# Both routers with the gate weights stationary, the output bias of the experts on VectorE, row transfers without holds, and the output stored by group

## The reference

```
logits = xf @ router_w.T
probs = jax.nn.sigmoid(logits.astype(jnp.float32))
topw, sel = jax.lax.top_k(probs, TOP_K)
combine = jnp.sum(topw[:, :, None] * onehot, axis=1)
h = jnp.square(jax.nn.relu(jnp.einsum('td,edw->tew', xf, W1e)))
out = jnp.einsum('ted,te->td', jnp.einsum('tew,ewd->ted', h, W2e), combine)
```

```
gates = jax.nn.softmax(xf @ wg, axis=-1)
idx = jnp.argmax(gates, axis=-1)
keep = loc < cap
disp = zeros.at[slot].set(xf, mode='drop')
h = jnp.einsum('ecd,edf->ecf', disp, w1) + b1[:, None, :]
y = jnp.einsum('ecf,efd->ecd', h, w2) + b2[:, None, :]
out = jnp.where(keep[:, None], gate_val[:, None] * y[slot], 0.0)
y2 = _ln(y1 + out, ln2_g, ln2_b)
```

## Time and profile before

| | |
|---|---|
| median of 3 runs | 2754.14 us |
| the profiled execution | 2750.36 us, of it 2748.6 us from the first to the last record (the span) |
| TensorE (PE) busy | 2386.5 us, 87% |
| its weight loads (PEld) | 1706.0 us, 62% |
| VectorE (DVE) busy | 1222.7 us, 44% |
| ScalarE (ACT) busy | 1013.9 us, 37% |
| GpSimd (POOL) busy | 146.0 us, 5% |
| mean granted TensorE clock | 0.959 of 2.4 GHz |
| DMA | 74.82 MB, 27 GB/s over the span |

### The profile page before, as it was taken

One profiled execution on the slowest core, in us unless ns is written; L12 is line 12 of the kernel. 1 busy time (PEld: TensorE's weight loads), 2 busy tenths in 40 slices (PEclk: granted clock), 3 DMA queues, 4 the chain that ended last, 5 costly groups with the idle time before them and its releaser, 6 DMA issues. The chain is left out here.

```text
span 2748.6 us, 38901 instructions
## 1 busy us (share of the span) xinstructions
PE 2386.5 (87%) x15301; PEld 1706.0 (62%) x15301; DVE 1222.7 (44%) x2353; ACT 1013.9 (37%) x2866; POOL 146.0 (5%) x238
## 2 busy tenths in 40 slices
PE   6778887999988999989999999978998997874894
PEld 4455655666655666666666666656876765654773
DVE  5456665777764434333333333345344443331003
ACT  3245564777762111113333333343223443331122
POOL 0000000000000000000000000021001000002003
PEclk8989999999999999999999999999999999996996
DMA  3000001000002000020000000000001000012332
GB/s 113 16 1 1 1 1 39 13 24 13 24 11 82 1 1 0 1 109 8 8 9 9 8 9 1 1 28 1 0 25 57 16 9 16 1 57 75 115 119 65
DMA packets 52535, 74.82 MB, mean 27 GB/s; under 512 B 8051, under 2 KB 41349, under 8 KB 51205
## 3 DMA queue, kind: packets, MB, share of 16 engines
q1 hardware_dynamic: 50820, 68.14, 7.4%
q0 software_dynamic: 1536, 4.20, 0.6%
HBM read 63.94 MB, written 8.39 MB: 26 GB/s over the span
## 5 line engine op out<-in xcount | busy, mean ns | idle before, releaser
L856 ACT ACTIVATE ca_prob<-bank,ca_nmax 128x512 f32<-128x512 f32 x256 | 174.0, 690 | 93.1 <-DVE ca_nmax L922 93.1
L922 DVE TENSOR_REDUCE ca_nmax<-bank 128x1 f32<-128x512 f32 x256 | 164.2, 683 | 56.3 <-PE bank L714 56.2
L856 ACT ACTIVATE na_prob<-bank,na_nmax 128x257 f32<-128x257 f32 x256 | 117.9, 473 | 180.9 <-DVE na_nmax L922 180.9
L1446 PE MATMUL bank<-XN,rf_W 128*128 128x512 f32 x384 | 171.8, 598 | 0.0
L1457 PE MATMUL bank<-rf_W,rf_h 128*128 128x256 f32 x768 | 170.8, 379 | 0.0
L1457 PEld LDWEIGHTS bank<-rf_W,rf_h 128*128 128x128 f32 x768 | 145.9, 190 | 33.1 <-issue 14.8
L728 PEld LDWEIGHTS bank<-cst,ca_prob 128*128 128x128 f32 x1024 | 112.3, 142 | 73.7 <-issue 63.3
L856 ACT ACTIVATE ra_prob<-bank,ra_nmax 128x256 f32<-128x256 f32 x256 | 118.2, 482 | 104.1 <-DVE ra_nmax L922 104.1
L1501 ACT ACTIVATE rf_r<-bank 128x512 f32<-128x512 f32 x96 | 57.4, 598 | 255.3 <-PE bank L1446 255.3
L728 PE MATMUL bank<-cst,ca_prob 128*128 128x128 f32 x1024 | 140.5, 279 | 6.6 <-DVE ca_pT L928 5.9
L922 DVE TENSOR_REDUCE na_nmax<-bank 128x1 f32<-128x257 f32 x256 | 90.8, 417 | 118.2 <-PE bank L714 118.2
(11 more groups left out here) (399 smaller groups left out, 4505.8 us busy)
## 6 DMA issues: line engine op xcount, KB each, us to landing
xl_w<-in_L_ffn_w SPq DMA_DIRECT2D x16, 1024.0 KB
dp_cx<-in_ctx_tok SPq DMA_DIRECT2D x4, 1024.0 KB, 14.8
ca_v<-in_ctx_values SPq DMA_DIRECT2D x8, 512.0 KB, 4.5
rf_W<-in_L_ffn_w SPq DMA_DIRECT2D x8, 512.0 KB, 8.7
na_Wkv<-in_L_xattn_Wkv SPq DMA_DIRECT2D x1, 4096.0 KB
na_cxT<-in_ctx SPq DMA_DIRECT2D x8, 512.0 KB, 3.4
ma_cxT<-in_ctx SPq DMA_DIRECT2D x8, 512.0 KB, 3.4
X<-in_x SPq DMA_DIRECT2D x1, 2048.0 KB, 7.6
```

The lines of the kernel that those rows point to most:

```text
L856: e = act.activation(prob[:, n % 2, u, hh * keys:(hh + 1) * keys], S[u][:, hh * keys:(hh + 1) * keys], ACT.Exp, bias=nmax[:, n % 2, u, hh: ...
L922: v.tensor_reduce(nmax[:, n % 2, u], S[u][:, 0:W].rearrange("p (h k) -> p h k", h=per), AX.X, ALU.max, negate=True).then_inc(maxed, 1)
L1446: mm = pe.matmul(g.bank[n % 3][:], W1[:, k, c * P:(c + 1) * P], g.XN[:, k, gi * GT:(gi + 1) * GT], start=(k == 0), stop=(k == KD - 1))
```

## The change

1. **Routed feed-forward.** The router weights are loaded into a tile of 32 columns that GpSimd has filled with zeros (SP waits for that fill, `blank`, before its first load). One `route()` for all tokens: the weights are the stationary side, 512 tokens the moving one, and group gi goes to the partitions 32 gi of bank 4. ScalarE copies the bank to `lgT`, TensorE transposes it after `hidden(0)` (`turn_logits`), and one `take()` gives the exponentials of all groups. The three later `route` calls are gone.
2. **Expert layer, gate.** The same form (`lgT`, its four transposes after q = 1); ScalarE takes `pe8` after five row copies instead of after two.
3. **Expert layer, bias.** b2 is loaded as 128 equal rows (128 KB instead of 1 KB for each expert) and added by VectorE where it copied before; the 16 bias products are gone.
4. **Expert layer, SP.** The loads for expert e + 2 wait for VectorE's copies of expert e (semaphore yc), not for TensorE's products (yp).
5. **Sends.** GpSimd waits once for all row copies and issues 16 indirect DMAs in a row, with one hold ahead of them.
6. **Output.** The last norm's SP block stores each group of 512 tokens when GpSimd has added it; `end_layer` now stands behind the store.

```diff
@@ layer_norm_phase
+                if store is not None:
+                    stored = g.sem(f"{tag}_stored")
+                    for gi in range(NG):
+                        sp.wait_ge(added, KD * (gi + 1))
+                        sp.dma_start(part(feature_rows(store), gi), part(dst, gi)).then_inc(stored, 16)
+                    sp.wait_ge(stored, 16 * NG)
@@ routed_ffn_layer, TensorE
-                def route(gi):
-                    if gi >= 2:
-                        pe.wait_ge(added, KD * (gi - 1))
-                    elif gi == 1:
-                        pe.wait_ge(taken, 1)
-                    for t in range(4):
-                        for k in range(KD):
-                            mm = pe.matmul(BR[:, t * E:(t + 1) * E], g.XN[:, k, gi * GT + t * P:gi * GT + (t + 1) * P],
-                                           Wr[:, k], start=(k == 0), stop=(k == KD - 1))
+                def route():
+                    for k in range(KD):
+                        for gi in range(NG):
+                            mm = pe.matmul(g.bank[4][32 * gi:32 * gi + 32, :], Wr[:, k], g.XN[:, k, gi * GT:(gi + 1) * GT],
+                                           start=(k == 0), stop=(k == KD - 1), skip_group_check=True)
                     mm.then_inc(logits, 1)
+                def turn_logits():
+                    pe.wait_ge(laid, 1)
+                    for j in range(4):
+                        mm = pe.transpose(BR[:, j * P:(j + 1) * P], lgT[:, j * P:(j + 1) * P], ident)
+                    mm.then_inc(lg_turned, 1)
...
-                route(0)
+                route()
                 hidden(0)
+                turn_logits()
                 for i in range(NI):
...
-                    if e == 3 and gi + 1 < NG:
-                        route(gi + 1)
@@ expert_layer, SP
                     for e in range(E):
+                        sp.wait_ge(yc, 2 * e + 2)
                         if e + 2 < E:
-                            sp.wait_ge(yp, 2 * e + 2)
                             load_weights(sp, e + 2)
                             load_rows(sp, e + 2)
-                        sp.wait_ge(yc, 2 * e + 2)
@@ expert_layer, GpSimd
+                    po.wait_ge(row_copied, TT // 2)
+                    hold_pool(g, po).then_inc(held, 1)
                     for t in range(TT):
-                        po.wait_ge(row_copied, t // 2 + 1)
-                        hold_pool(g, po).then_inc(held, 1)
                         po.indirect_dma_start(sent, bass.IndirectOffsetOnAxis(ap=slot[:, t:t + 1], axis=0), rows[:, t], None)\
                           .then_inc(sent_all, 16)
-                        po.wait_ge(held, t + 1)
@@ expert_layer, TensorE, out
-                            pe.matmul(g.bank[5 + t][:, 0:D], g.c("ones")[0:1, :], b2[:, e % 2], start=True, stop=False)
@@ expert_layer, VectorE
-                            v.tensor_copy(yt[:, e % 2, t], g.bank[5 + t][:, 0:D]).then_inc(yc, 1)
+                            v.tensor_tensor(yt[:, e % 2, t], g.bank[5 + t][:, 0:D], b2[:, e % 2], ALU.add).then_inc(yc, 1)
```

More of the change, by code:

```diff
@@ L144, in build @@
         if STAGES >= 8:
-            position_attention_layer(g)
+            position_attention_layer(g, out)
             end_layer()
-        store_phase(g, out)
 def hold_pool(g, po):
@@ L171, in _ @@
             v.memset(g.onesb[:], 1.0).then_inc(made, 1)
[L174 to L181, removed]
 def layer_norm_phase(g, tag, src=None, dst=None, gain=None, shift=None, resid=None, rms_gain=None, eps=None,
-                     prefetch=None, prepare=None, by_position=False, loaded=None, aside=None):
+                     prefetch=None, prepare=None, by_position=False, loaded=None, aside=None, store=None):
     nc = g.nc
@@ L1501, in rectify @@
                         act.activation(r[:, n % 3], g.bank[n % 3][:], ACT.Relu).then_inc(relu, 1)
-                take(0)
+                act.wait_ge(logits, 1)
+                act.activation(lgT[:], g.bank[4][:], ACT.Copy).then_inc(laid, 1)
                 rectify(0)
[L1505 to L1510, removed]
+                take()
+                for i in range(1, NI):
+                    rectify(i)
             @block.vector
@@ L2193, in _ @@
                     pe.wait_ge(wl, 48)
-                    for t in range(TT):
-                        for k in range(KD):
-                            mm = pe.matmul(g.bank[0][:, t * E:(t + 1) * E], g.XN[:, k, t * P:(t + 1) * P], Wg[:, k],
-                                           start=(k == 0), stop=(k == KD - 1))
+                    for k in range(KD):
+                        for gi in range(NG):
+                            mm = pe.matmul(g.bank[0][32 * gi:32 * gi + 32, :], Wg[:, k], g.XN[:, k, gi * GT:(gi + 1) * GT],
+                                           start=(k == 0), stop=(k == KD - 1), skip_group_check=True)
                     mm.then_inc(lp, 1)
                     for q in range(TT // 2):
+                        if q == 2:
+                            pe.wait_ge(laid, 1)
+                            for j in range(4):
+                                mm = pe.transpose(g.bank[3][:, j * P:(j + 1) * P], lgT[:, j * P:(j + 1) * P], ident)
+                            mm.then_inc(lg_turned, 1)
                         if q >= 4:
@@ L2360, in _ @@
                     v.wait_ge(merged, TT // 2)
-        layer_norm_phase(g, "nxl", src=g.XN, dst=g.X, gain=gain, shift=shift, resid=g.X)
+        layer_norm_phase(g, "nxl", src=g.XN, dst=g.X, gain=gain, shift=shift, resid=g.X, store=out)
 HOST_T = ("L1_xattn_w_qkv", "L1_xattn_w_proj", "L1_ffn_router_w", "L3_xattn_W_src", "L3_xattn_W_tgt", "L3_xattn_W_out",
```

80 lines of the change are left out of this document (47 added, 33 removed).

## The result

The changed kernel takes 2725.78 us (median of 4 runs, 2713.53 to 2734.20) where the kernel before takes 2753.45 on the same chip (4 runs). The ratio is 0.9896, with a 95% interval of 0.9857 to 0.9935. A second set of runs of it gave 2731.99 and 0.9917 (0.9892 to 0.9942). The time forecast, 2730, lies between; the profiled span fell from 2748.6 to 2724.0.

The account below looks back on a forecast made before the run. TensorE was taken to bound the routed feed-forward, a chain of engines and DMA the expert layer; -4.7 - 9.3 - 1.4 - 4.7 - 4.2 = -24.3 us gave 2729.8, forecast 2730 us, range 2719 to 2742.

Parts of the forecast that it names:

- Routed layer, -4.7: Routed feed-forward: three route calls go (-5.1 us), four new transposes cost 0.44 us; sum -4.7 us.
- what leaves its list is gained in full: Routed feed-forward: TensorE is the bound, 78.00 us of work in a 78 us window, so removed work is saved time.
- The rival of the clock: Dense route and gate keep TensorE's clock high: 1.6 us in the routed layer, 2 more in the expert layer; 2726, chance 0.2.
- Front, -9.3: Expert layer, gate's start to GpSimd's hold ahead of the first send: 22.9 us before, gain 8.1 to 10.5, middle 9.3.
- the first of the two cases worked out: Expert layer, full clock behind the gate: hold 12.4 us after the gate's start, against 14.8 at half clock.
- Sends, -1.4: Expert layer's sixteen sends: without holds between them 1.29 us apart instead of 1.39; -1.4 us, between 0 and 2.1.
- Loop, -4.7: Expert loop: 16 bias products go (-10.1 us), SP's wait and b2's load add 0.9 us in each of six rounds.
- The rival in which the loop gives its gain back: Expert loop: rows delayed by 2 us instead of 0.9, low clock through all w2 products; 15.6 us back, 2746, chance 0.08.
- Output, -4.2: Kernel's end, last add to end of span: 8.5 us becomes 4.3; -4.2 us, between -3 and -5.4.
- The column groups overlap: Gate and route; the rival said no overlap at 512 columns: gate 13.7 us, route 6.9, time 2744, chance 0.05.
- the 4.5 us that the prediction estimated beside its sum for the gate: Expert layer's gate: by the skill's rule on weight loads sharing rows, about 4.5 us rather than 3.6.
- b2 does not crawl: Expert loop; the rival said broadcast b2 uses one DMA engine, 5.6 us ahead of the rows: +31 us, 2761, chance 0.02.

Follow-up runs that it names:

- idle products: Products of 8 columns, results unused, at the routed layer's end: 22 with the new route alone 1.0017, 42 in the kernel before 1.0093, 22 with rows early 0.9837.
- the one moved load: Changed kernel with SP loading the rows of expert e + 2 once TensorE has turned expert e's rows, ahead of the weights: 2692.24 us, ratio 0.9768.

## Why the prediction was right, and where not

- **The sum and its parts.** 24.3 us were forecast; the profiled spans differ by 24.6, the two timed ratios say 28.6 and 22.9. The parts are not those of the sum.
- **Routed layer, -4.7.** This term failed, by the sentence "what leaves its list is gained in full". In its own segment the layer gained more than was set: 370.0 to 372.5 us in the three executions with the old route and no idle products, 361.9 to 366.1 in the eight with the new one, 8.0 less in the mean. The rival of the clock is in these numbers and gives nothing in the whole. Where the first expert ran at full clock the segment takes 361.9 to 363.5 and the next stage 630.9 to 631.0; where it did not they take 366.0 to 366.1 and 627.0 to 627.5. Both together are 992.7 to 994.4 in all eight, and 999.4 to 999.8 with the old route.

  The stages behind give the gain back, measured from the routed layer's norm in the means of the same eight and three. At the masked attention's norm 5.9 us of the 8.0 are left, at its end 2.3 (1465.3 against 1467.6). In it a packet of instructions falls on the start of the first context load in all eight executions with the shifted stream and in the one that shifts it with idle products: load 5.1 to 5.8 us, stage 235.6 to 238.1 (in two of the nine SP's issue came 1.5 us later too). In five without it the load takes 3.8 to 4.3 us and the stage 232.9 to 235.0. The runs with idle products show both ways that the place of the stream brings the packet and the late load. They did not bring the gain back in the time: with the products the routed segment itself is 4.3 to 8.5 us longer.

  Behind that, the position attention takes 172.8 us in the mean with the new route and 172.9 with the old, but moves between 162.6 and 179.7 with the low clock (windows at the end), so that 2.3 us can't be seen in one execution. In the time the layer alone measured 0 (-4 to +3 us), and leaving it out of the change costs nothing (0.9915 against 0.9917 and 0.9896).
- **Front, -9.3.** 9.9 to 10.2 us; full clock behind the gate, the first of the two cases worked out.
- **Sends, -1.4.** 26.7 to 25.1 us from the hold to the first turned rows: 1.6.
- **Loop, -4.7.** The mechanism held; its sizes moved. The bias products, 10.1 in the sum, are worth 12.3, because the products behind each one are slower too. SP's wait costs 0.48 (0.45 set), b2's load 0.6 to 1.0 a round (0.45 set); six rounds at 1.15 give back 6.9, where 5.4 were set. At full clock that would leave -5.4. Over executions the clock decides: sends and loop took 209.3, 205.8, 209.5 and 209.2 us with the old loop and 206.3, 197.7 and 195.9 with the new, 8.5 less in the mean, or 6.9 without the sends. The low clock came in 5, 3 and 2 of six rounds of the new loop (5, 4, 4 and 5 of the old), although its idle time is longer; the prediction had counted on five, at worst on all six. The rival in which the loop gives its gain back is nearly met by one execution (206.3) and not by the mean; a second b2 load is enough for it (209.9).
- **Output, -4.2.** From the last add to the end 8.5 us became 4.4 (4.3 set), 4.1 less.
- **The other rivals.** The column groups overlap: 16 products of 512 columns in 1.93 us at full and 3.64 at half clock, against 6.9 and 13.7 if they did not; the 4.5 us that the prediction estimated beside its sum for the gate did not come either. b2 does not crawl: at most 1.0 us for its 128 KB, not 5.6.

So the number was right in part by luck: the routed term, 4.7 us of it, was worth 2.3 by the traces and nothing by the times, and the other terms made up for it. They gave 10.1 + 1.6 + 6.9 + 4.1 = 22.7 us where 19.6 were set, and the expert layer alone measured 23.4 (1 - 0.9915, of 2751.5).

## What to carry to other kernels

Ask of a load that a waiting engine needs when its buffer is free, not behind what it has stood so far: here the one moved load was worth 40 us (2692 against 2732; 25 to 33 of them seen in sends and loop), more than the whole change. A gain in a stage is a gain in the time only if the untouched stages behind it stay as they were; cut the traces at the same events, several executions of each kernel, and run the part alone. A stage that waits, even for 2 us, may pay once more in clock, so a saved wait can be worth more than its length: six of 3.1 us are 19, and taking them away gave 25 to 33.

## What the runs showed of the hardware

- An instruction packet of 16.4 KB that starts 1.0 to 1.3 us behind the issue of a load of 2 x 512 KB made it land in 5.1 to 6.2 us, the mean of its halves, instead of 3.8 to 4.3 (17 loads against 11, the first context loads of two stages, no exception). Beside single loads of 512 KB, 2.4 to 3.3 us behind the issue, it made no difference: 3.2 to 3.6 us in 38 loads, 3.1 to 3.8 in 130 without. So its place in the load counts. In the loop of the kernel before, the one round with such a packet among its loads had the idle time of 3.31 us where the others had 1.84 to 2.01; but the longest of the changed kernel's second execution, 3.72, has none among its loads.
- Products of 8 columns with 128 x 128 weights cost 0.11 us each at full clock (4.97 us for 44), as much as a transpose of 128 columns. In the series of 84 the granted clock fell to the lower level while TensorE ran them one behind the other, and the second half took 0.21 us each; windows over the two halves:

```profile
1185.40:1190.40 5.00, 5.00 (x43) 4.97 (x42) 0.88 (x2) 0.00 (x0) 0.00 (x0) 0.92 0.01 3
1190.40:1199.40 9.00, 9.00 (x43) 9.00 (x44) 0.00 (x0) 0.00 (x0) 0.00 (x0) 0.50 0.00 0
```

- The position attention, untouched, in the changed kernel and in the one with the routed layer alone:

```profile
2290.10:2452.70 162.60, 128.50 (x896) 94.80 (x897) 57.05 (x128) 47.91 (x176) 6.42 (x15) 0.98 0.03 7
```

```profile
2289.10:2468.20 179.10, 145.86 (x900) 107.21 (x904) 57.24 (x128) 48.42 (x176) 6.46 (x15) 0.87 0.02 7
```
